# Input statistics two tiles at a time, weights in halves, three rotation slots, latents by the staging tile, and the first attention loop entered in steps

## The reference

```
h = layernorm(x);  q = h @ wq (16 heads x (128 + 64));  ckv, k_pe = h @ wkv_a (64 + 64)
ckv = rmsnorm(ckv) * kv_norm_scale;  k_nope, v = ckv @ wkv_b (16 heads x (128 + 128))
q_pe, k_pe = rope(q_pe), rope(k_pe)
attn = softmax(causal((q_nope.k_nope + q_pe.k_pe) * 192**-0.5)) @ v
x = x + layernorm(attn @ wo)
x = x + layernorm(shared_expert(h2) + sum of the top 2 of 16 experts(h2)),  h2 = layernorm(x)
```

## Time and profile before

| | us |
|---|---|
| median of 3 timed runs | 1417.64 (1416.69 to 1423.31) |
| profiled execution | 1431.8 |
| its span, first to last instruction | 1430.0 |
| busy in the span: PE / DVE / ACT / POOL | 1196.9 / 827.4 / 812.3 / 733.4 |
| input stage (until the last tile's low part ends) | 0 to 39.5 |
| heads' loop | 39.9 to 74.3 |
| projection blocks (to the last spread) | 74.7 to 136.6 |
| entry into attention (to the first Exp) | 136.6 to 151.3 |

### The profile page before, as it was taken

One profiled execution on the slowest core, in us unless ns is written; L12 is line 12 of the kernel. 1 busy time (PEld: TensorE's weight loads), 2 busy tenths in 40 slices (PEclk: granted clock), 3 DMA queues, 4 the chain that ended last, 5 costly groups with the idle time before them and its releaser, 6 DMA issues. The chain is left out here.

```text
span 1430.0 us, 20120 instructions
## 1 busy us (share of the span) xinstructions
PE 1196.9 (84%) x6856; PEld 580.2 (41%) x6861; DVE 827.4 (58%) x1834; ACT 812.3 (57%) x1252; POOL 733.4 (51%) x444
## 2 busy tenths in 40 slices
PE   2986788999999779989999879999999998488710
PEld 2532345444434623333333443333333335366510
DVE  4566466666566655555555755656656615655444
ACT  2644464565665255657566447777777784265521
POOL 0046332345555235656666528777778785235453
PEclk9998899999999989999999989999999999799965
DMA  9024100100001010000001101000000000256742
GB/s 276 16 67 107 49 1 1 44 21 17 23 23 37 16 44 12 20 8 16 16 16 30 31 12 51 13 12 23 23 23 23 1 23 16 58 153 186 181 129 92
DMA packets 61207, 68.17 MB, mean 48 GB/s; under 512 B 9728, under 2 KB 51968, under 8 KB 60800
## 3 DMA queue, kind: packets, MB, share of 16 engines
q1 hardware_dynamic: 55056, 54.16, 13.3%
q0 software_dynamic: 4864, 10.51, 3.2%
q10 hardware_dynamic: 1200, 2.38, 0.6%
HBM read 37.50 MB, written 14.83 MB: 37 GB/s over the span
## 5 line engine op out<-in xcount | busy, mean ns | idle before, releaser
L529 POOL TENSOR_TENSOR D<-D,B 128x1024 f32<-128x1024 f32 (+3 forms) x256 | 513.3, 2005 | 175.6 <-ACT B L704 158.9
L1047 DVE TENSOR_REDUCE mxp<-ps 128x1 f32<-128x512 f32 (+3 forms) x640 | 385.9, 610 | 319.2 <-PE ps L1551 212.6
L704 ACT ACTIVATE B<-ps 128x1024 f32<-128x1024 f32 (+1 forms) x320 | 286.3, 895 | 238.1 <-PE ps L1576 166.4
L1592 PE MATMUL ps<-B,kv 128*64 128x512 f32 (+3 forms) x1280 | 305.4, 557 | 11.8 <-ACT C L604 10.9
L604 ACT ACTIVATE ps<-D 128x1024 f32<-128x1024 f32 (+1 forms) x320 | 287.6, 899 | 31.4 <-DVE D L1060 17.8
L1576 PE MATMUL ps<-A,KTh 128*128 128x512 f16 (+3 forms) x768 | 210.6, 357 | 3.9 <-ACT ps L604 3.9
L522 POOL TENSOR_TENSOR D<-B 128x1024 f32<-128x1024 f32 (+1 forms) x32 | 71.0, 2220 | 242.3 <-ACT B L704 242.3
L1551 PE MATMUL ps<-KTh,A 128*128 128x512 f16 (+3 forms) x384 | 137.0, 359 | 3.2 <-DVE mxp L1047 3.0
L1576 PE MATMUL ps<-A,KTl 128*128 128x512 f16 (+3 forms) x384 | 136.6, 356 | 0.0
L1592 PEld LDWEIGHTS ps<-B,kv 128*64 128x64 f32 x1280 | 64.1, 135 | 103.2 <-issue 75.9
L1576 PEld LDWEIGHTS ps<-A,KTh 128*128 128x128 f16 x768 | 63.8, 98 | 102.6 <-issue 55.9
(11 more groups left out here) (256 smaller groups left out, 1893.0 us busy)
## 6 DMA issues: line engine op xcount, KB each, us to landing
results<-B SPq DMA_DIRECT2D x64, 128.0 KB
xnTl<-in_L_ffn_experts_gate_up SPq DMA_DIRECT2D x16, 256.0 KB, 2.7
A<-in_L_attn_wq SPq DMA_DIRECT2D x1, 3072.0 KB, 26.2
B<-in_L_attn_x SPq DMA_DIRECT2D x5, 512.0 KB, 6.3
D<-in_L_attn_wo SPq DMA_DIRECT2D x1, 2048.0 KB, 31.5
A<-C SPq DMA_DIRECT2D x32, 64.0 KB, 2.0
A<-stg SPq DMA_DIRECT2D x16, 128.0 KB, 2.3
A<-stg SPq DMA_DIRECT2D x64, 32.0 KB, 1.9
```

The costliest lines, as they stand in the source:

```text
L529: nc.gpsimd.tensor_tensor(acc[:, :, c0:], acc[:, :, c0:], Pr[:, kt % P_RING, :, c0:], ALU.add).then_inc(sum_done, 1)
L704: nc.scalar.activation(Pr[:, kt % P_RING, :, c0:], ps[:, 2 * (kt % ST_RING):2 * (kt % ST_RING) + 2, c0:], ACT.Exp, scale=SM_SCALE).then_in ...
L1047: V.tensor_reduce(mxp[:, s, i4, kc:kc + 1], ps[:, BK_X + j % MX_RING, 0:w], AX.X, ALU.max).then_inc(mx_free, 1)
L1592: ins = T.matmul(ps[LORA * s:LORA * (s + 1), BK_O, c0:], kv[:, kt, 0:LORA], Pr[:, kt % P_RING, s, c0:], start=(kt == 0), stop=(kt == KT - 1))
```

## The change

Statistics, root and reciprocal of tiles 4 to 15 are made in the tile loop, two tiles at a time. The identity comes with a DMA of its own, first on ScalarE's queue; wq, wo and wkv_b come in halves of eight heads, each with its semaphore. All latents of blocks 0 to 7 go through the staging tile, both heads of a pair, with one 128-row instruction on ScalarE and on the vector engine and two DMAs. The rotation slots are three (`rot_of`), the third in D. The maxima of the first pair come 3, 3 and 2 in blocks 4 to 6; the spreads stand in block 7 after `project(7, 0)`, the second in bank 6 (`spread_bank`). `prime` is in two steps. The last `rot_high`s stand behind the first two Exps, and the wait for all moves becomes one wait per pair ahead of `values_out`. Two Exps and the first widen of pair 1 wait for the rotation slots that they overwrite.

```diff
-        first_rot = B[:, :].rearrange("p (r i q) -> p r i q", r=2, i=4)
+        first_rot = [[m[:, a + i * CQ:a + (i + 1) * CQ] for m, a, i in where_] for where_ in (
+            [(B, 0, i) for i in range(4)], [(B, 4 * CQ, i) for i in range(4)],
+            [(D, 2 * CQ, 0), (D, 2 * CQ, 1), (D, 6 * CQ, 0), (D, 6 * CQ, 1)])]
...
+        def spread_bank(qc, p, s):
+            return BK_O if qc == p == 0 and s else BK_M
+        def first_units(G):
+            return [range(0), range(0, 3), range(3, 6), range(6, 8), range(0)][max(G - NG + 1, 0)]
...
+        def rot_of(G):
+            return first_rot[(G + 1) % 3]
...
-            sp.dma_start(wq_raw, wq.rearrange("(k p) (h c) -> p k h c", p=P, c=QH)).then_inc(in_wq, 16)
-            sp.dma_start(wo_raw, wo.rearrange("(h p) e -> p h e", p=P)).then_inc(in_wo, 16)
+            for a in range(2):
+                hs = slice(a * H // 2, (a + 1) * H // 2)
+                for k in range(KE):
+                    sp.dma_start(wq_raw[:, k, hs], ...[:, hs]).then_inc(in_wq[a], 16)
+                sp.dma_start(wo_raw[:, hs], wo.rearrange("(h p) e -> p h e", p=P)[:, hs]).then_inc(in_wo[a], 16)
...
                 for s in range(2):
-                    if s == 0 and G < 2 * NG:
-                        continue
...
+            act.dma_start(c32[:, 0:P], c32_d[:, 0:P]).then_inc(in_ident, 16)
...
-            act.wait_ge(var_ready, 1)
-            nc.scalar.activation(std[:, :], var[:, :], ACT.Sqrt).then_inc(std_ready, 1)
+            def first_root(k, tiles):
+                act.wait_ge(var_ready, k + 1)
+                nc.scalar.activation(std[:, tiles], var[:, tiles], ACT.Sqrt).then_inc(std_ready, 1)
+            first_root(0, slice(0, TC))
             for t in range(NT + 1):
...
+                if t % 2 and t + TC - 1 < NT:
+                    first_root((t + 1) // 2, slice(t + TC - 1, t + TC + 1))
...
-                if G < 2 * NG:
-                    copy(qt(G // NG, G % NG * HG + 2 * i, 0)[0:LORA], ps[0:LORA, bank, :], 1 / WS)
-                    copy(stage_of(G, i)[LORA:, 0], ps[LORA:, bank, :], 1 / WS).then_inc(lat_hi, 1)
-                else:
-                    copy(stage_of(G, i)[:, 0], ps[:, bank, :], 1 / WS).then_inc(lat_hi, 1)
+                copy(stage_of(G, i)[:, 0], ps[:, bank, :], 1 / WS).then_inc(lat_hi, 1)
...
                 act.wait_ge(pv_done, CR_PV + first_kt(qc) + (p + 1) * tiles_of(qc))
+                if qc == 0:
+                    act.wait_ge(*moved(2 * NG - 2 + p // 4, p % 4))
                 copy(OT[:, bass.ds(p * CQ, CQ)], ps[:, BK_O, :]).then_inc(o_free, 1)
...
+                    if qc == p == 0 and kt in (0, 2):
+                        act.wait_ge(rot_lo, 4 * NG - 4 + kt)
                     nc.scalar.activation(Pr[...], ps[...], ACT.Exp, scale=SM_SCALE).then_inc(exp_done, 1)
+                    if qc == p == 0 and kt in (0, 1):
+                        rot_high(2 * NG - 1, kt)
...
-            for G in range(2 * NG + 1):
+            for G in range(2 * NG):
...
-                else:
-                    for i in range(4):
-                        act.wait_ge(*moved(2 * NG - 2, i))
-                        act.wait_ge(*moved(2 * NG - 1, i))
...
-            for g in range(NC):
-                dve.wait_ge(in_x[g], 16)
-                moments(xs, (g + 1) * TC, first=g * TC)
-            inv_std(NT, LN_EPS)
+            dve.wait_ge(in_x[0], 16)
+            moments(xs, TC)
+            inv_std(TC, LN_EPS)
...
                 if t + 2 < NT:
                     normalise(t + 2)
+                if t % 2 == 0 and t + TC < NT:
+                    dve.wait_ge(in_x[t // TC + 1], 16)
+                    moments(xs, t + TC + 2, first=t + TC)
+                    variance(t + TC + 2, LN_EPS, first=t + TC)
+                if t % 2 and t + TC - 1 < NT:
+                    one_over(t + TC + 1, first=t + TC - 1)
...
-                if G >= 2:
-                    dve.wait_ge(rot_lo, 2 * G - 2)
+                if G >= 3:
+                    dve.wait_ge(rot_lo, 2 * G - 4)
...
+                if (qc, p) == (0, 1):
+                    dve.wait_ge(rot_lo, 4 * NG)
-                V.tensor_copy(minus_m[:, p % 2, s, :], ps[:, BK_M, :]).then_inc(wide_done, 1)
+                V.tensor_copy(minus_m[:, p % 2, s, :], ps[:, spread_bank(qc, p, s), :]).then_inc(wide_done, 1)
...
             for G in range(2 * NG):
-                for i in range(2):
-                    lat_low(G, i, i)
+                lat_low(G, 0, 0)
+                if G == 2 * NG - 1:
+                    for s in range(2):
+                        widen(0, 0, s)
+                lat_low(G, 1, 1)
                 first_turns(G)
-                if G >= NG:
-                    j0 = 2 * (G - NG)
-                    for j in (j0, j0 + 1):
-                        maxima(0, 0, j)
-                    if G == NG + 3:
-                        widen(0, 0, 0)
-            widen(0, 0, 1)
+                for j in first_units(G):
+                    maxima(0, 0, j)
...
-            pe.wait_ge(in_const, 32)
+            pe.wait_ge(in_ident, 16)
...
                     project(G, b, b)
-                if G >= NG:
-                    j0 = 2 * (G - NG)
-                    for j in (j0, j0 + 1):
-                        max_unit(0, 0, j)
-                    if G == NG + 3:
-                        spread(0, 0, 0)
-            pe.wait_ge(wide_done, 1)
-            spread(0, 0, 1)
+                    if b == 0 and G == 2 * NG - 1:
+                        for s in range(2):
+                            spread(0, 0, s)
+                for j in first_units(G):
+                    max_unit(0, 0, j)
             pe.wait_ge(lat_lo, 4 * NG)
+            prime(0)
             pe.wait_ge(x_free, 4 * NG)
-            prime()
+            prime(1)
```

More of the change, by code:

```diff
@@ L57 @@
 NEG = -1e30
+ROOTS = 2 + (NT - TC) // 2
 OUT_PARTS = [(g, j, j + TC // 2) for g in range(NC) for j in (0, TC // 2)]
@@ L198, in attention_moe @@
         BK_X, BK_O, BK_M = 4, 6, 7
-        in_const, in_wa, in_wq, in_wkvb, in_wo = map(sem, ("in_const", "in_wa", "in_wq", "in_wkvb", "in_wo"))
+        in_ident, in_const, in_wa = map(sem, ("in_ident", "in_const", "in_wa"))
+        in_wq, in_wkvb, in_wo = ([sem(f"{name}_{a}") for a in range(2)] for name in ("in_wq", "in_wkvb", "in_wo"))
         in_x = [sem(f"in_x_{g}") for g in range(NC)]
@@ L284, in moved @@
             if G < 2 * NG:
-                return q_moved[G % 2 * 4 + slot], (G // 2 + 1) * (16 if slot < 2 else 64)
+                return q_moved[G % 2 * 4 + slot], (G // 2 + 1) * (32 if slot < 2 else 64)
             return q_moved[8 + slot], (G - 2 * NG + 1) * (32 if slot < 2 else 128)
@@ L532, in rotated @@
             def rotated(G):
-                q = first_rot[:, G % 2]
+                q = rot_of(G)
                 pool.wait_ge(x_free, 2 * G + 2)
-                nc.gpsimd.tensor_tensor(q[:, 0], q[:, 0], q[:, 1], ALU.subtract).then_inc(rot_done, 1)
-                nc.gpsimd.tensor_tensor(q[:, 2], q[:, 2], q[:, 3], ALU.add).then_inc(rot_done, 1)
+                nc.gpsimd.tensor_tensor(q[0], q[0], q[1], ALU.subtract).then_inc(rot_done, 1)
+                nc.gpsimd.tensor_tensor(q[2], q[2], q[3], ALU.add).then_inc(rot_done, 1)
             def rotated_low(G):
@@ L598, in _ @@
             act.dma_start(biasb[:, :], bias.rearrange("(a c) -> a c", a=1).broadcast_to([P, NE])).then_inc(in_wa, 16)
-            act.dma_start(c32[:, :], c32_d[:, 0:C_END]).then_inc(in_const, 16)
+            act.dma_start(c32[:, P:], c32_d[:, P:C_END]).then_inc(in_const, 16)
             act.dma_start(c16[:, :], c16_d.bitcast(BF16)).then_inc(in_const, 16)
-            act.dma_start(wkvb_raw[0:LORA], wkv_b.rearrange("c (h n) -> c h n", h=H)).then_inc(in_wkvb, 16)
+            for a in range(2):
+                hs = slice(a * H // 2, (a + 1) * H // 2)
+                act.dma_start(wkvb_raw[0:LORA, hs],
+                              wkv_b.rearrange("c (h n) -> c h n", h=H)[:, hs]).then_inc(in_wkvb[a], 16)
             def copy(dst, src, scale=1.0):
@@ L643, in _ @@
                     if g == PE_AFTER:
-                        act.wait_ge(in_wq, 16)
+                        for a in range(2):
+                            act.wait_ge(in_wq[a], 16 * KE)
                         for k in range(KE):
@@ L749, in _ @@
             act.wait_ge(wfl_done, H)
-            for G in range(2 * NG + 1):
+            for G in range(2 * NG):
                 for i in range(2):
-                    if G < 2 * NG:
-                        lat_high(G, i, i)
+                    lat_high(G, i, i)
                 for i in range(2):
@@ L902, in _, with variance, one_over @@
             roots = [0]
-            def inv_std(n, eps, scale=1.0, src=None, first=0):
+            def variance(n, eps, scale=1.0, src=None, first=0):
                 src = mv[:, first:n, 1] if src is None else src
                 V.tensor_scalar(var[:, first:n], src, scale, eps, ALU.mult, ALU.add).then_inc(var_ready, 1)
```

(19 more changed lines are left out.)

38 lines of the change are left out of this document (17 added, 21 removed).

## The result

Before 1417.16 us (median of 4 runs), after 1384.43 us (4 runs): ratio 0.9752, 95% interval 0.9721 to 0.9783, so 32.7 us less. The profiled execution of the changed kernel took 1384.2 us, span 1382.4. The forecast was 1398.7, a gain of 18.9 us, and its range ended at 1388: the sign was right, the size some 14 us too small.

What follows compares the result with a forecast made beforehand. It took the input stage, the 7.38 us turn chain and the entry's wait on SyncE's moves as bounds, with SyncE's queue binding next. 3.6+15.3=18.9 us off 1417.64 gave 1398.7 us, range 1388 to 1408.

Steps and rivals of the forecast that it cites:

- Statistics, 3.6 us: Input stage: statistics two tiles at a time put the last mean subtraction at 35.5 instead of 39.12 us, 3.6 us gained.
- Weights in halves, 0: Input DMAs: halves bring 0 by themselves; without them the statistics part could lose up to some tenths.
- Queue of issues as the new bound: Projection loop: SyncE's 12 issues a block, 7.5 to 7.8 us, take the place of the 7.38 us turn chain.
- Entry, 15.3: Entry into attention: waits per slot instead of for all moves start the first Exp earlier, 15.3 us gained.
- A: Projection loop: the queue does not bind, engines set the entry, seeds at 126.6, 4.2 us sooner, 1394.5; chance 0.18.
- B: Input stage gives nothing, through a slower matrix engine clock or root waits; gain 15.3, 1402.3 us; chance 0.13.
- D: SyncE's queue: issues without a pause each take longer, slower than before; 1424 us at 1.1 us an issue; chance 0.04.
- C: Projection blocks: matrix engine loses its clock waiting for lat_high; two blocks cost 10.4 us, 1409; three, 1414; chance 0.11.
- the added half move: Latent staging: pure cost by the skill's rule, which alone would give back about 9 us of the queue's time.
- Nothing later depends on absolute time, so it passes to the end: Code after the changed stretch: the whole gain of 18.9 us reaches the end of the kernel.
- The 18.9 us of the sum: Whole change: 3.6 us from the input stage plus 15.3 us at the entry into attention.
- I take the same difference off both: Whole time: 18.9 us off both profile and median, giving about 1412.9 us and 1398.7 us.

Runs made afterwards that it cites:

- e15: Kernel before with only the statistics two tiles at a time, DMAs and semaphores as before: ratio 0.9931.
- e14: Kernel before with the identity on its own DMA, the weights in halves and the semaphores these need, statistics as before: ratio 0.9922.
- e17: Kernel before with each odd head's latent move in its first loop split in two, twelve issues a block instead of ten: ratio 0.9952.
- e18: Changed kernel, but ScalarE waits for all moves ahead of the first pair, as in the kernel before: ratio 0.9884.
- e7: Changed kernel with 16 scatters moved, one behind each pair's sum in the third and fourth group of queries, none left out: ratio 0.9692.
- e9: Changed kernel with the even heads' latents written straight to their place in the first loop, ten DMAs a block instead of twelve: ratio 0.9823.
- e10: Changed kernel with four extra loads of a quarter of x ahead of the first, so everything runs some 20 us later: ratio 0.9914.
- e8: Kernel before with four more waits on the matrix engine ahead of the heads' loop, on a semaphore already at its value: ratio 1.0032.
- e11: Kernel before with extra waits early on ScalarE and the vector engine (24 in all), on semaphores already at their value: ratio 0.9968.
- e13: Kernel before with four unused semaphores declared among the first, so later ones have numbers four higher: ratio 0.9999.
- e1: Kernel before, unchanged, profiled once more: span 1417.5 us.

## Why the prediction was wrong

*Statistics, 3.6 us: right for the part.* Alone they brought 3.9 us against the mean of the nine traces with the old input stage (39.2 to 35.27, e15). The whole front brought 5.3 between the two first profiles and some 4.8 over all traces with it (33.58 to 35.72).

*Weights in halves, 0: not shown to be wrong.* Alone with the identity the last low part came at 36.71 (e14), 2.5 us below the mean and 0.7 below the lowest of the nine. In that trace the last quarter of x is waited for 2.24 us, in the nine 1.85 to 6.03. A quarter of wq and the second half of wo are issued only at 18 us (the issue before them takes most of the 13.42 us row above), so fewer bytes may travel beside x; that x lands sooner for this reason I only argue. I had looked only at when the weights are needed.

*Queue of issues as the new bound: right.* 12 issues a block, 7.6 us, seeds at 126.2 (130.8 less 3.6 was the forecast, 127.2), by the same waits; e17 and e18 give the same queue. The 56 issues took 36.9 us, 0.660 each, with the one of 1.69 in them (36.6 was the forecast), and began at 87.3 (88.6).

*Entry, 15.3: right.* The first Exp is 20.8 us earlier, less 5.3 for the front makes 15.5; counted at the second pair's seed it is 16.4. I had the table load after the first scores; it runs beside them.

*Rivals.* A, B and D did not happen. (The terms of A add up to seeds at 126.2, not 126.6, and 4.6 us.) C happened in part. Block 5 lost the clock for eight matmuls after 2.58 us of waiting, for a maximum and not for `lat_high` as C has it; the queue hid this. The clock was 0.50 between 125 and 131 us too: in e7 it was 1.00 there, and counted from the last low part the first Exp came 1.4 us sooner and the second pair's seed 0.4. It was C in full in e9. Against direct writes the change's half moves are cheaper by 9 us (e9), with the 16 DMA engines busy 0.61 of the time from 95 to 137 us. By the rule on partition halves (the Trainium skill, DMA: Bandwidth & Descriptors, Rules for kernel authors) I had priced the added half move as pure cost. The rule compares two halves with one transfer over 128 partitions, which no run here has; e9 has one half by DMA and writes the other by the engines.

*The failing step: "Nothing later depends on absolute time, so it passes to the end".* The 18.9 us of the sum stand beside 19.5 once the scatters are left out, and 26 where they are spread, both uncertain by some 6. What I took for equal was the shared code: two bursts of scatters cost the kernel before 20 to 22 us in its traces and the changed one 6 to 9, some 14 us less, which is what the forecast lacked. "I take the same difference off both" failed by itself, for the profile alone (1412.9 forecast, 1384.2 measured): the profile of the kernel before was long by 12.5 us against its second one, 8.7 of it in the final gathers, and the changed kernel's first profile had the short form of these. The sign was there to be seen: 7.94 us "remote" after the last matmul of a group, with every engine idle, was a row of the trace of before that my slices never opened, because the diff did not touch it.

What stays open is why the burst costs less after the change. Not the moment (e10), not the place of the code of one engine (e8, e11), not the numbers of the semaphores alone (e13), not the number of DMAs alone (e17, whose bursts were 4 to 6 us of 20 cheaper). The identity and the weights by DMAs of their own go with the cheaper first burst in every trace; the DMA for the identity and the halves were not tried apart. I have no mechanism for it. That the hold comes from the scatters, and goes when they are spread, is shown.

## What to carry to other kernels

Where a queue of issues is full, look for what waits for its end, not for what feeds it: a wait for each slot at its first use was worth 18 us (e18 against the changed kernel), the faster engines ahead of it nothing by themselves. Before passing a gain to the end, read every all-idle gap of the profile, in the parts that the diff leaves alone too: a wait that the profile gives to nobody can change size with any edit. Issue indirect scatters of single words one at a time between other work, not in a burst before a point at which all engines meet.

## What the hardware showed that I had not expected

Eight indirect scatters of 128 words, 4 bytes each, are issued in 10 us, but their completions take 21 to 32 us from the first issue, and for 6 us at a time no semaphore update of any engine gets through (500.0 to 505.9 in e1, 7.6 us in e3), so that a finished matmul is signalled 11.2 us late. One scatter for each pair, 34 us or more apart, costs nothing that can be seen (e7). The Trainium skill (DMA: Bandwidth & Descriptors, Specifications) says that below 512 bytes the DMA engine reads, modifies and writes back; no run here shows whether that is the reason.

Sixteen further DMAs, more than 300 us ahead of the scatters, made the kernel before 6 us faster (e17); why is open. And taking 16 issues, 10 us of them, out of the full queue made the kernel 9 us slower (e9). Of these, 2.9 us come with waits of 4.91 and 2.85 us, after each of which the matrix engine went on at 1.2 instead of 2.4 GHz.
